# Waits that other waits imply are taken out of a decoder-layer kernel, and VectorE's four one-element copies with them

## What is computed

```python
x = x + attention(layernorm(x))              # 16 heads of 8, rope, causal
x = x + cross_attention(layernorm(x), ctx)   # ctx: 64 x 77 x 128
x = x + ffn(layernorm(x))
# ffn: 8 router logits per token; the largest probability picks one of 7 experts (or none)
#   routed = down_e(up_e(x) * silu(gate_e(x))), shared = the same with one shared expert
#   result = 2 * top1_probability * routed + shared
```

## Time and profile before

| | |
|---|---|
| median of 3 runs | 1093.27 us (1092.92 to 1093.52) |
| the profiled execution's own time | 1091.68 us |
| its span | 1089.3 us |
| busy, of the span | PE 1007.5 (92%), PEld 859.1, DVE 852.5 (78%), ACT 744.4, POOL 628.8 |
| phase one's hardware loop, 48 steps | 203.7 to 790.9 us, 12.23 us per step |
| phase two's tiles | about 884 to 1075 us |
| granted TensorE clock, mean | 0.986 |

### The profile page before, as it was taken

How to read it: one execution, slowest core, us unless ns; L and a number is a source line. 1 busy time by engine, 2 the same in 40 slices (tenths; PEclk the granted TensorE clock), 3 DMA queues, 4 the chain that set the end, 5 groups by cost and what they waited for, 6 DMA issues and landing times.

```text
span 1089.3 us, 49897 instructions
## 1 busy us (share of the span) xinstructions
PE 1007.5 (92%) x16232; PEld 859.1 (79%) x16233; DVE 852.5 (78%) x2853; ACT 744.4 (68%) x1557; POOL 628.8 (58%) x1488
## 2 busy tenths in 40 slices
PE   2689999999999999999999999999998879999995
PEld 1567788778877788777877788777877879999995
DVE  3357889888888888888888888888885557777774
ACT  0367887888878887888878888888864235555552
POOL 0345767667667766677667766776654214444443
PEclk9899999999999999999999999999999989999998
DMA  5222110001000100001000100011100122222220
GB/s 130 66 70 71 28 37 26 26 28 33 25 25 25 35 26 25 25 29 32 25 25 25 36 25 25 25 31 32 28 23 20 49 76 70 74 71 65 70 69 5
DMA packets 66661, 44.41 MB, mean 41 GB/s; under 512 B 24135, under 2 KB 61451, under 8 KB 66592
## 3 DMA queue, kind: packets, MB, share of 16 engines
q1 hardware_dynamic: 55424, 30.35, 10.3%
q0 software_dynamic: 5312, 12.18, 3.3%
q10 hardware_dynamic: 5856, 0.99, 0.6%
HBM read 23.96 MB, written 18.29 MB: 39 GB/s over the span
## 4 chain that ended last, share of the span: by engine, by line
PE 64%; SPq 12%; DMA 11%; issue 3%; ACT 2%; DVE 2%; POOL 1%; ACTq 0%; DVEq 0%; POOLq 0%
SPq L391 11%; DMA arena<-arena 10%; PE pv L1198 6%; PE scores L1383 6%; PE scores L1388 6%; PE ro L1400 6%; PE scores L1247 5%; PE scores L1240 5%; PE ro L1255 4%; PE scores L1110 4%; PE ro L1207 4%; PE pj L1307 3%; PE scores L1102 3%; PE st L1311 2%; ACT arena L913 2%
## 5 line engine op out<-in xcount | busy, mean ns | idle before, releaser
L991 ACT ACTIVATE arena<-scores 128x1024 f32<-128x1024 f32 (+1 forms) x256 | 260.6, 1019 | 56.5 <-PE scores L1110 36.2
L668 DVE TENSOR_REDUCE arena<-scores 128x8 f16<-128x1024 f32 (+1 forms) x256 | 255.1, 997 | 35.8 <-PE scores L1084 25.6
L913 ACT ACTIVATE arena<-st 128x128 f16<-128x128 f16 (+2 forms) x256 | 155.2, 606 | 22.0 <-PE st L1311 7.7
L1198 PE MATMUL pv<-arena 128*32 128x128 f32 (+1 forms) x4096 | 139.2, 277 | 0.3 <-issue 0.3
L913 ACT ACTIVATE arena<-arena 128x512 f16<-128x512 f32 (+2 forms) x192 | 93.0, 485 | 45.7 <-DVE arena L717 40.0
L448 POOL TENSOR_TENSOR arena<-arena,neg_half 128x1 f32<-128x1 f32 x192 | 106.4, 554 | 29.1 <-POOL arena L439 10.9
L1198 PEld LDWEIGHTS pv<-arena 128*32 128x32 f32 (+1 forms) x4096 | 104.7, 110 | 13.9 <-issue 1.1
L549 POOL DMA_INDIRECT out_dram<-x_tile x70 | 69.4, 992 | 38.4 <-POOL carried L548 26.1
L518 POOL DMA_INDIRECT xs<-pay,put x64 | 69.3, 1083 | 27.3 <-issue 27.3
L867 DVE SCALAR_TENSOR_TENSOR half_hid<-tanh_s,scores 128x512 f32<-128x512 f32 x70 | 48.1, 687 | 40.9 <-ACT tanh_s L1040 40.9
L1311 PE MATMUL st<-id,arena 128*128 128x128 f16 (+1 forms) x1024 | 73.9, 215 | 4.7 <-POOL arena L477 4.3
(11 more groups left out here) (175 smaller groups left out, 2658.1 us busy)
## 6 DMA issues: line engine op xcount, KB each, us to landing
x_tile<-xs SPq DMA_DIRECT2D x70, 129.0 KB, 2.1
arena<-arena SPq DMA_DIRECT2D x512, 4.0 KB
arena<-in_x_dram SPq DMA_DIRECT2D x64, 64.0 KB
out_dram<-pay SPq DMA_DIRECT2D x64, 64.0 KB, 1.6
arena<-in_ctx_dram SPq DMA_DIRECT2D x64, 38.5 KB
w_gate<-in_L_ffn_gate_w_dram SPq DMA_DIRECT2D x7, 256.0 KB, 2.8
w_up<-in_L_ffn_up_w_dram SPq DMA_DIRECT2D x7, 256.0 KB, 3.1
w_down<-in_L_ffn_down_w_dram SPq DMA_DIRECT2D x7, 256.0 KB, 3.7
```

Source lines behind the costliest of these rows:

```text
L668: v.tensor_reduce(nmax[:, n, :].rearrange("p (m r s) -> p r m s", r=2, s=SLOT)[:, u, :, 0:HG], pair(s)[:, :, 0:HG * keys].rearrange("p m ( ...
L913: return a.activation(to, of, ACT.Copy)
L991: a.activation(e32[0:rows, 2 * n + u, :], scores[0:rows, 1024 * s:1024 * (s + 1)], ACT.Exp).then_inc(sexp_done[n][u], 1)
L1198: last = t.matmul(pv[SLOT * j:SLOT * (j + 1), 0:2 * P].rearrange("p (c a y) -> p a c y", a=2, y=SLOT)[:, a], vals[0:rows, p, at0:at0 + SLO ...
```

## The change

Some 80 of 180 calls of `wait` go, on all five engines, and most of the users in the lists of `turn` on TensorE. Each was for an event that another wait, at the same place or earlier in the same queue, already implies; the remaining waits and the events are as they were. Some of the cut diff (the whole has the same kind of line for every piece):

```diff
@@ SyncE
             def load_ctx(b, p):
-                wait(sync, ctxT_psum, b - 1)
@@ GpSimd
                 wait(pool, ln_mv[n], b + 1)
-                wait(pool, ln_rstd[n], b)
...
             def scaled(b, p, n):
                 wait(pool, o_recip[n], b + 1)
-                wait(pool, oT_ready[n], b)
@@ ScalarE
             def nmT_copy(b, p, n):
                 wait(act, nmT_psum[n], b + 1)
-                wait(act, max_rows[n][p], 32 * b - 32 * p)
...
             def k2_high(b, p):
                 wait(act, k2_ready, b + 1)
-                wait(act, qkT2_psum, b - 1)
@@ TensorE
-                at(i, p, 8, project_out, 0, ((resid_done[1], -2),), ((logits_ready, -3),), ((xT_ready[2], -3),), ((q2_ready, 0),), ((sh_added, -4),), ((hot_posed, -4), (run_ready, -4)), ((xT_ready[1], 0),), ((resid_done[0], 0),))
+                at(i, p, 8, project_out, 0)
...
-                at(i, p, 9, cross_for_max, 1, 1, ((smax_done[1][0], 1),), ((sexp_done[1][0], 0),), ((smax_done[0][0], 3),), ((sexp_done[0][0], 2),), ((smax_done[1][1], 0),))
+                at(i, p, 9, cross_for_max, 1, 1)
```

On VectorE the copies go, and their waits are placed as pieces of their own in `step`, each ahead of the operation that stands ahead of the aggregation or the statistics:

```diff
-            def carry(n):
-                v.tensor_copy(carried[:, n:n + 1], eps[:, :])
@@ ln_stats_of
-                wait(dve, ln_mv[n], b)
-                if n == 2:
-                    carry(3)
                 v.bn_stats(bn6[:, n, :], rows).then_inc(ln_stats[n], 1)
+            def stats_seen(b, p, n):
+                wait(dve, ln_stats[n], b + 1)
+            def resid_seen(b, p):
+                wait(dve, resid_done[1], b + 1)
             def ln_mean_var(b, p, n):
-                wait(dve, ln_stats[n], b + 1)
-                wait(dve, ln_rstd[n], b - 1)
-                carry(n)
                 v.bn_aggr(mv[:, n, p, :], bn6[:, n, :]).then_inc(ln_mv[n], 1)
@@ step
+                at(i, p, 2, stats_seen, 0)
                 at(i, p, 3, row_max, 0, 1, 0)
                 at(i, p, 2, ln_mean_var, 0)
...
                 at(i, p, 7, add_cross)
+                at(i, p, 7, resid_seen)
                 at(i, p, 8, marks_of)
                 at(i, p, 7, ln_stats_of, 2)
...
+                at(i, p, 7, stats_seen, 2)
                 at(i, p, 8, hot_of)
                 at(i, p, 7, ln_mean_var, 2)
...
                 at(i, p, 4, ln_stats_of, 1)
+                at(i, p, 4, stats_seen, 1)
+                at(i, p, 8, gate_of)
                 at(i, p, 4, ln_mean_var, 1)
-                at(i, p, 8, gate_of)
                 at(i, p, 8, add_shared)
```

More of the change, by code:

```diff
@@ L763, in put_of @@
                 wait(dve, hot_posed, b + 1)
-                wait(dve, scattered[place(b, p)], sent(b, p))
                 v.tensor_copy(put[:, place(b, p):place(b, p) + 1], put_f[:, :]).then_inc(put_ready, 1)
@@ L1113, in cross_exp_round, with self_for_max @@
                     last.then_inc(sexp_psum[1][u], 1)
-            def self_for_max(b, p, u, s, now, *before):
+            def self_for_max(b, p, u, s, *users):
                 wait(pe, qkT_ready, b + 1)
-                turn(pe, b, now, *before)
+                turn(pe, b, *users)
                 for h in range(4):
@@ L1185, in two_turns, with values @@
                         round2(s2, u2, p2, g)
-            def values(b, p, n, now, *before):
+            def values(b, p, n, *users):
                 vals, rows = ((val, P), (val2, C))[n]
-                wait(pe, sexp_done[n][0], b + 1)
                 wait(pe, sexp_done[n][1], b + 1)
-                wait(pe, (val_ready, val2_ready)[n], b + 1)
-                turn(pe, b, now, *before)
+                turn(pe, b, *users)
                 for g in range(HG):
@@ L1249, in shared_up, with shared_down @@
                 last.then_inc(sh_up, 1)
-            def shared_down(b, p, now, *before):
+            def shared_down(b, p, *users):
                 wait(pe, sh_hid, b + 1)
-                turn(pe, b, now, *before)
+                turn(pe, b, *users)
                 for c in range(FC):
@@ L1285, in busy_pj, with positions @@
                     t.matmul(pj[:, c * P:(c + 1) * P], w_qkv[:, 0:P], w_qkv[:, 0:P], start=True, stop=True)
-            def positions(b, p, now, *before):
+            def positions(b, p, *users):
                 wait(pe, hot_ready, b + 1)
-                wait(pe, run_ready, b)
-                turn(pe, b, now, *before)
+                turn(pe, b, *users)
                 cols = ro[:, 2 * P:2 * P + 2 * E].rearrange("p (n e) -> p n e", n=2)
```

156 lines of the change are left out of this document (41 added, 115 removed).

## The result

The changed kernel takes 1082.92 us (median; 1081.95 to 1084.67) against 1093.1 us (1092.17 to 1093.52) for the kernel before in the same measurement: ratio 0.991, 95% interval 0.9893 to 0.9927. The forecast was 1085.3 us in a range of 1075.0 to 1092.5. The profiled execution took 1082.73 us, its span 1080.6; with the 1091.68 and 1089.3 of before that is 8.9 us less.

A forecast was written before the change was run, and what follows sets the result against it. Each loop step was taken as TensorE's run to L1333 plus the DMA chain back to L1110. Gains 3.6 + 3.6 + 0.3 + about 0.5 = 8.0 us, off the profiled 1091.68, gave 1083.7, median 1085.3 us, range 1075 to 1092.5.

The forecast's parts named there:

- The bound: Phase two closed; a loop step lasts TensorE's run L1110 to L1333 plus the wait chain back to L1110.
- The chain, 0.06 us a step: ScalarE's queue wait before its copy of the transposed maxima goes: 0.06 us (0 to 0.09), 60 steps, 3.6 us.
- TensorE's run, 0.15 us a pair: L1110 to L1333: thinner queues save 0.12 us in one step, 0.03 in the other; 24 pairs, 3.6 us.
- the two thirds of 0.18: Of the 0.18 us by which every second run is longer, 0.12 goes, with 0.11 of the excess at L1207 to L1247.
- the same in both: Sign of being right: L1207 to L1247, 0.22 and 0.33 us before, takes equal time in both steps.
- VectorE's copies, nothing on the path: Four copies, 0.28 us a step, hidden by VectorE's wait of about 1.1 us for the router's logits; costed at nothing.
- The moved waits, all in slack: VectorE's marks start 0.13 us later, statistics 0.06, first row_max up to about 0.07; all within VectorE's slack.
- The sum: 3.6 + 3.6 + 0.3 = 7.5 us, plus about 0.5 for the ramps: 8.0 us.
- slower: Rival: VectorE's new waits delay L745, so L1293 waits; 0.11 us in each of 60 steps, 1100 us; chance 0.07.

The follow-up runs named there:

- nm_back: Changed kernel with one wait put back, for max_rows at ScalarE's copy of cross attention's row maxima: 1085.7 us.
- only_dve: Kernel before with VectorE's edits alone (four copies gone, waits thinned and moved): 1091.3 us.
- copies_back: Changed kernel with all four of VectorE's one-element copies put back, without their waits: 1088.3 us.
- only_act: Kernel before with the edits to ScalarE alone: 1089.5 us against 1093.0.
- back_early: Changed kernel with VectorE's transposition for w_o ahead of the third norm's statistics and the moved wait taken off the marks: 1082.6 us.
- row_by_act: Changed kernel with one of SyncE's four DMAs for cross attention's row maxima issued by ScalarE: ratio 0.992 to the kernel before.
- scatter_low_row: Changed kernel, w_o transposition before third norm's statistics, one row-maxima DMA issued by ScalarE, GpSimd's scatter behind low halves of q and k: 1079.75 us.
- copy_aggr0: Changed kernel with one VectorE copy back, ahead of the first norm's aggregation, without a wait: ratio 0.9934 to the kernel before.

## Why the prediction was right where it was, and where it was not

**The bound.** Right: phase two did not move, L1038 waits for the DMAs in all 48 steps, and a step is run plus chain. What was missing is that the run is not TensorE's alone. It has a wait in its middle, at w_o, that ends with a path through GpSimd and VectorE, and what lies on that path is no slack of either engine.

**The chain, 0.06 us a step.** Right in mechanism, and shown by the reversal of this one wait in nm_back; it measured 0.10 and 0.08, about the upper bound of 0.09. Over 24 pairs that is 4.2 us in the loop, where the sum had 2.9.

**TensorE's run, 0.15 us a pair.** It came to 0.08, but not from where the prediction placed it. L1207 to L1247 still takes 0.24 and 0.32 us: the two thirds of 0.18 did not go, and "the same in both" is wrong. The first step's gain of 0.11 is 0.05 between the other product of that line and the gate product (417.93 to 418.26 before, 415.85 to 416.13 after) and 0.04 behind L1169; only_dve shows both, so they come from VectorE's side and not from TensorE's own queue. The 24 waits of TensorE a step that I counted as a thinner queue left no mark that I can find, though TensorE's part alone was not run; copies_back, which has it, comes to the same loop as only_act, which has not (585.4 and 585.2). In the second step L1169 starts 0.025 later than before, which I put down to the marks' moved wait; back_early has L1169 back at its old place, but it takes that wait off and moves the transposition at once, and so doesn't part the two.

**VectorE's copies, nothing on the path.** This is the step that failed. I took the wait for the logits, 1.1 us a step, as a cover for all that VectorE does. It covers only what stands ahead of it in the order and is needed behind it. Two of the four copies are not so: that ahead of the statistics stands behind the wait and in front of the transposition, and that ahead of the first norm's aggregation feeds GpSimd, which has no such wait. Back in the kernel they cost 0.06 to 0.07 us a step each where they count, together 4.2 us in the loop (copies_back, 585.4 against 581.2), the 0.07 of the order that the earlier trace rows had for each. VectorE's edits together are worth only 0.8 us of the loop (only_dve, 586.4 against 587.2), far less than the copies cost in the changed kernel; the next part has the likely reason.

**GpSimd's queue, no term in the sum.** The second path has wait instructions of its own, and the change takes some of them out. Two stood between the variance and the power of the first norm. First the kernel before, then the changed one, in the first kind of step:

```profile
413.85 0.19 POOL L439 TENSOR_TENSOR arena<-arena,eps 128x1 f32<-128x1 f32 x1 [0.37 <-DVE arena L650]
414.20 0.55 POOL L448 TENSOR_TENSOR arena<-arena,neg_half 128x1 f32<-128x1 f32 x1 [0.17 <-POOL arena L439]
...
416.25 1.08 POOL L518 DMA_INDIRECT xs<-pay,put  x1 [0.42 <-issue]
```

```profile
411.74 0.19 POOL L436 TENSOR_TENSOR arena<-arena,eps 128x1 f32<-128x1 f32 x1 [0.32 <-DVE arena L624]
412.00 0.55 POOL L438 TENSOR_TENSOR arena<-arena,neg_half 128x1 f32<-128x1 f32 x1
...
414.02 1.08 POOL L496 DMA_INDIRECT xs<-pay,put  x1 [0.37 <-issue]
```

The power starts 0.17 us behind the variance before and 0.08 after, and the pause ahead of the scatter goes from 0.43 to 0.37 us, as means of the 48 steps: the row is 0.15 us a step shorter. only_act and only_dve still have 0.17 and 0.43, and every kernel made from the changed one that leaves the scatter in its place has 0.08 and some 0.37. That fits the part of the gain that only_act and only_dve lack: with ScalarE's part alone the chain gets shorter and GpSimd's row does not. But no kernel has GpSimd's part alone, or ScalarE's, VectorE's and GpSimd's together, so it is read from traces and not shown by a run.

**The moved waits, all in slack.** Half wrong. Counted from the context scores, the marks start 0.07 us later than before in the first kind of step and 0.11 in the second, against 0.13 foreseen; that is as much as the copy behind them gave, or more. In the first kind of step it costs next to nothing, since GpSimd's scaled output holds the marks either way: they end 3.30 us after the context scores with the wait, and 3.29 in back_early without it, though they start there at 2.88. In the second kind they end at 3.25 and 3.13, and of this 0.12 us TensorE feels the 0.025 named above, at most.

**The rest.** VectorE's busy time was to fall by 35 us and fell by 1.1 in the loop and 4.7 in all: the copies overlapped their neighbours (0.15 us long, 0.07 of the order), and without them the neighbours don't. The wait for the logits was to grow and fell by 7.8 us in the loop; the steps are 6 us shorter in all, and VectorE's own busy time in them hardly changed. The sum had 6.5 us for the loop and 1.5 for all else; the profiled executions show 6.0 in the 48 steps and 2.6 behind them up to the last router product. In the loop the chain's term was 1.3 us too small and the run's 1.7 too large, which nearly cancels. The forecast was 2.4 us too high: 1.0 us because the pieces outside the loop gave 2.9 us and not 1.5, which no run explains, less the 0.5 that the loop fell short; and 1.4 because the sum started from a profiled execution 1.6 us under its median, where that of the changed kernel lay only 0.2 under its own. That it was so near is partly luck, and more so since the copies were put at nothing. Of the rivals, "slower" named the wrong place (nothing waits at the positions, L1214, for the hot experts), but a moved wait may reach TensorE at w_o, with 0.025 us in every second step and not the 0.11 in every step that it priced.

## What to carry to other kernels

A wait of an engine covers only what is ahead of it in that engine's order and has no reader on another engine before it; ask of each removed operation who is first to feel it, and follow that engine's row until it pauses. Where a kernel is tuned, several paths have nearly one length: shortening one alone gives back a part (only_act), an edit that undoes one shows less than its length (nm_back), the same work moved to another engine can make the other path longer (row_by_act), and the next path appears as soon as two are shorter (scatter_low_row). A wait instruction in a queue costs time where its engine's row is such a path, and not by how many there are: the one of ScalarE in the chain gave 0.08 to 0.10 us a step (nm_back), TensorE's 24 a step left no mark. Judge such edits by the loop's own steps, since the ramps differ by more than the edit.

## What was not expected of the hardware

VectorE's marks, an operation with two SBUF inputs, got longer wherever they began with more than some 0.2 us of GpSimd's scaled output left, and then ended 0.02 to 0.03 us after it: 0.30 us in the changed kernel, 0.37 in copy_aggr0, 0.41 in row_by_act, against 0.22 where less of it was left. No wait shows in the profile for this, only a longer duration. The Trainium skill, "SBUF — State Buffer", section "Who interferes with whom", says that a VectorE instruction with two SBUF inputs contends with a GpSimd instruction that reads SBUF, that the shared port pair is an exclusive lock, and that issue order decides who blocks. These rows agree. Here 0.1 us in the start of the marks decides whether they are held.

ScalarE and SyncE take the same time to issue a DMA here, 0.66 and 0.64 us, and GpSimd's indirect one takes 1.08 us with 0.37 idle ahead of it. The Trainium skill's "VectorE: DVE Perf Modes", section "The DRAIN you can't avoid", has it from a chain of eight copies that a semaphore behind each costs nothing. Here a wait for the operation right ahead put the marks 0.11 us behind where they started when they could begin inside it (in the second kind of step, 3.02 us after the context scores and not 2.91; 2.91 again in back_early, where that wait is gone). So for this pair of short operations the runs do not agree, and the measurement decides.
